# Fifteen filler products from a tile set by DVE, in place of ten that need POOL's identity

## What is computed

```python
# x: (8, 128, 32, 32); Wq, Wk: (64, 128); Wv: (128, 128)
xf = x.reshape(b, c, n)                                  # n = 1024 pixels
q = einsum('oc,bcn->bon', Wq, xf) + bq[None, :, None]
k = einsum('oc,bcn->bon', Wk, xf) + bk[None, :, None]
v = einsum('oc,bcn->bon', Wv, xf) + bv[None, :, None]
attn = softmax(einsum('bci,bcj->bij', q, k), axis=-1)
out = einsum('bcn,bmn->bcm', v, attn)
return gamma * out + x
```

## Time and profile before

| what | us |
|---|---|
| median of 3 runs | 231.02 |
| lowest and highest of them | 230.31, 231.49 |
| the profiled execution's own time | 231.92 |
| its span, first to last instruction | 230.1 |
| PE busy | 223.4 (97% of the span) |
| ACT, POOL, DVE busy | 177.9, 189.1, 168.2 |
| mean granted clock of TensorE | 0.999 |

### The profile page before, as it was taken

The page is one execution under the profiler, slowest core; times in us unless marked ns, Lnnn a source line. Parts: engine busy times, 40 slices in busy tenths (PEclk is TensorE's granted clock), DMA queues, the critical chain, the costliest instruction groups (busy, mean ns, idle before and its releaser), DMA issues.

```text
span 230.1 us, 5324 instructions
## 1 busy us (share of the span) xinstructions
PE 223.4 (97%) x1858; PEld 204.8 (89%) x1858; DVE 168.2 (73%) x339; ACT 177.9 (77%) x342; POOL 189.1 (82%) x163
## 2 busy tenths in 40 slices
PE   7999989999999999999999999999999999999994
PEld 4477868999999999999999999999999999999994
DVE  0586869976878878868897778768887777776544
ACT  2578967777887888877887788878887878878980
POOL 8668888696998979987798979989799878799871
PEclk9999999999999999999999999999999999999999
DMA  5571940096406770195504961076302951100111
GB/s 151 143 265 28 203 137 4 2 229 166 157 3 160 159 231 0 15 232 133 178 0 93 226 171 63 2 184 141 140 0 35 231 153 43 47 0 3 46 50 46
DMA packets 17978, 24.56 MB, mean 107 GB/s; under 512 B 9760, under 2 KB 10784, under 8 KB 17952
## 3 DMA queue, kind: packets, MB, share of 16 engines
q1 hardware_dynamic: 17520, 24.03, 40.9%
q10 hardware_dynamic: 432, 0.20, 0.3%
HBM read 8.72 MB, written 4.19 MB: 56 GB/s over the span
## 4 chain that ended last, share of the span: by engine, by line
PE 88%; DVE 5%; ACT 2%; DMA 2%; issue 1%; SPq 1%; POOL 0%; POOLq 0%; ACTq 0%
PE sums L612 24%; PE scores L592 13%; PE scores L593 12%; PE work L548 12%; PE sums L626 12%; PE work L542 5%; DMA k_hilo<-qk_lo 2%; DVE neg_max L840 2%; PE work L535 1%; PE scores L641 1%; PE work L537 1%; PE work L536 1%; PE work L641 1%; PE sums L632 1%; DVE weight_lo L878 1%
## 5 line engine op out<-in xcount | busy, mean ns | idle before, releaser
L469 POOL TENSOR_TENSOR weight_lo<-weight,weight_hi 128x512 bf16<-128x512 f32 x97 | 134.9, 1406 | 22.3 <-ACT weight_hi L779 21.5
L840 DVE TENSOR_REDUCE neg_max<-work 128x1 f32<-128x512 f32 x120 | 81.4, 683 | 4.7 <-PE work L548 4.7
L776 ACT ACTIVATE weight<-scores 128x512 f32<-128x512 f32 x128 | 76.7, 599 | 9.5 <-PE scores L593 1.8
L612 PEld LDWEIGHTS sums<-values,weight_hi 128*128 128x128 f32 x504 | 76.8, 189 | 5.0
L612 PE MATMUL sums<-values,weight_hi 128*128 128x258 f32 x504 | 80.7, 282 | 0.0
L779 ACT ACTIVATE weight_hi<-scores 128x512 fp32r<-128x512 f32 x128 | 76.8, 600 | 0.0
L592 PE MATMUL scores<-q_hihi,k_hilo 128*128 128x256 f32 x256 | 71.0, 300 | 0.2 <-ACT q_lomax L760 0.2
L593 PE MATMUL scores<-q_lomax,k_hione 128*128 128x256 f32 x256 | 66.2, 281 | 0.0
L548 PE MATMUL work<-k_hilo,q_hihi 128*128 128x512 f32 x120 | 49.0, 413 | 0.8 <-DVE neg_max L840 0.5
L592 PEld LDWEIGHTS scores<-q_hihi,k_hilo 128*128 128x128 f32 x256 | 48.2, 188 | 1.6 <-issue 0.9
L593 PEld LDWEIGHTS scores<-q_lomax,k_hione 128*128 128x128 f32 x256 | 48.5, 189 | 1.1 <-issue 0.5
(11 more groups left out here) (72 smaller groups left out, 158.4 us busy)
## 6 DMA issues: line engine op xcount, KB each, us to landing
x_turned_sb<-in_x_turned SPq DMA_DIRECT2D x8, 512.0 KB, 5.0
out<-y_sb SPq DMA_DIRECT2D x15, 256.0 KB, 2.7
x_sb<-in_x SPq DMA_DIRECT2D x7, 512.0 KB, 4.4
q_hihi<-qk_hi SPq DMA_DIRECT2D x12, 256.0 KB, 4.4
q_lomax<-qk_lo SPq DMA_DIRECT2D x7, 256.0 KB, 5.7
k_hione<-qk_hi SPq DMA_DIRECT2D x7, 256.0 KB, 5.6
k_hilo<-qk_hi SPq DMA_DIRECT2D x6, 256.0 KB, 3.2
k_hilo<-qk_lo SPq DMA_DIRECT2D x6, 256.0 KB, 5.7
```

Of the source, the lines that this page charges most:

```text
L469: pool.tensor_tensor(weight_lo[:, r], weight[:, r], weight_hi[:, r], ALU.subtract).then_inc(weight_lo_pool_done, 1)
L612: last = pe.matmul(sums[:, u % 2 * PAIR + it, 0:VCOLS], weight_hi[:, r, part_tile(kt, it)], values[p][:, key_tile(s, kt)], start=(j == 0 a ...
L776: act.activation(weight[:, r], scores[:, s % 2], ACT.Exp)
L840: dve.reduce_max(neg_max[:, t, h:h + 1], place, AX.X, negate=True).then_inc(neg_max_done, 1)
```

## The change

The ten transposes of `identity` become fifteen plain fp32 products, each `filler.T @ filler` over 128 columns. `filler` is a new 128x128 fp32 tile of ones. DVE sets it with a memset ahead of everything else that it does, and counts a new semaphore, `filler_set`. PE's first wait is for that semaphore in place of POOL's second setup step. The fillers write the same PSUM place as before, which nobody reads before it is overwritten. POOL's setup, ACT's use of the identity and all that follows the fillers stay as they are.

```diff
-WARM_UP = 10
+WARM_UP = 15
...
         identity = sbuf("identity", [128, 128], fp32)
+        filler = sbuf("filler", [128, 128], fp32)
...
+        filler_set = sem("filler_set")
...
             def keep_busy(turns, place):
                 for _ in range(turns):
-                    pe.transpose(place[:, 0:128], identity[:, :], identity[:, :])
-
-            pe.wait_ge(pool_setup, IDENTITY_MADE)
+                    pe.matmul(place[:, 0:128], filler[:, :], filler[:, :], start=True, stop=True)
+
+            pe.wait_ge(filler_set, 1)
             keep_busy(WARM_UP, sums[:, 0])
...
+            dve.memset(filler[:, :], 1.0).then_inc(filler_set, 1)
             dve.wait_ge(biases_loaded, 16)
```

## The result

| | before | after |
|---|---|---|
| median, us | 230.86 (6 runs) | 232.43 (6 runs) |
| lowest to highest, us | 230.31 to 231.96 | 231.89 to 232.83 |
| ratio after to before | | 1.0058, 95% interval 1.0034 to 1.0082 |
| profiled execution: time, span | 231.92, 230.1 | 231.89, 230.1 |

The change costs 1.57 us by the medians, and 1.3 us (0.8 to 1.9) by the ratio. The two profiled executions show next to none of it: 231.92 and 231.89 us. Why that is so is the main thing to learn here. It has two parts: the moment at which TensorE's clock rose, and 0.25 us that the changed kernel does not lose at 107 us (under "Hidden elsewhere").

A forecast was written before the change was run, and what follows sets the result against it. PE bounds the kernel, busy 97% of the span. k0 starting 3.48 us later, less 2.06 us for six shorter passes, gives +1.42 us on the median 231.02: 232.4 us, range 230.9 to 233.1.

The forecast's parts named there:

- Hidden elsewhere: Rival: k0 late, but the stretch from 10 to 16 us gives most back; about 231.0 us, chance 0.08.
- The start: Head: DVE's memset, begun at 0.73, lets the first filler start at 0.98 instead of 1.52, 0.54 us earlier.
- The passes: Fillers on PE: fifteen fp32 products are 30 passes, 0.2125 us each cold, 6.38 us if all are cold.
- The rise: TensorE's clock doubles at 7.33 us; all 30 fillers cold to 7.36, six warm passes to 9.94, +1.42 us.
- the one lag of the trace: Head: the clock rises 6.35 us behind the first filler, transposes included, so at 7.33 after the change.
- the rival: Head: only plain products count for the clock, which rises at 4.97; +0.27 us, 231.3 us, chance 0.32.
- Two signs of failure: Head and end: the clock rises before 4.4 us, or the delay at k1 is not found again at the end.
- Profiled executions: Whole kernel: profiled 231.92 us would become 233.34; the median of the runs, 0.90 lower at 231.02, becomes 232.4.
- The argument against the rival: Head: the profiled execution, rise at 7.87, was slowest of four; 230.31 would mean a rise at about 4.7.
- theory A: Head: every PE pass, transposes too, counts for the clock; its rise varies between executions; loss is the 30 passes' time.
- theory B: Head: only plain products count for the clock, transposes do not; as a rival of the forecast 231.3 us, chance 0.32.
- the faster rival: Fillers: a product costs one pass, not two; 229.7 us; chance 0.08 together with a rise before 4.4 us.

The follow-up runs named there:

- e4: The changed kernel with its 15 fp32 products made one-pass (bf16, 256 columns): 230.72 us, ratio 0.9981 to the kernel before.
- e5: The changed kernel with 13 one-pass bf16 products instead of 15 fp32 ones: 230.57 us, ratio 0.9967 to the kernel before.
- e12: The changed kernel with PE's old wait for POOL's identity added, 15 fp32 products: 232.87 us, ratio 1.0093 to the kernel before.
- e2: The kernel before with ten fp32 products in place of its ten transposes, still waiting for POOL: 232.22 us, ratio 1.0049.
- e13: The changed kernel with 7 fp32 products instead of 15 and PE's old wait for POOL's identity added: ratio 1.0007 to the kernel before.
- e6: The changed kernel with 30 fp32 products instead of 15: 237.36 us, ratio 1.0282 to the kernel before.
- e7: The kernel before, unedited and profiled once more: 231.76 us, against 231.92 in its first profile.
- e1: The kernel before without any filler: 232.06 us, ratio 1.0039.
- e11: The changed kernel with ten one-pass bf16 products, waiting also for POOL's identity as the kernel before did: ratio 1.0014 to the kernel before.

## Why the prediction was right

**The start.** DVE's memset began at 0.83, not at 0.73, and took 0.17 us; the first filler came at 1.05 where I said 0.98 (bounds 0.88 to 1.13). Nothing on DVE was delayed. Right, and small.

**The passes.** Line 634 shows x30, cold 0.213 us apart and warm 0.11, as worked out from the earlier trace rows. e4 and e5 show that the second pass of each product is what the change loses. e12, e2 and e13 give its price: from 7 to 15 products behind POOL the ratio goes from 1.0007 to 1.0093, 2.0 us for 16 passes, 0.12 us each.

**The rise.** Here the working was right in its kind and wrong in one step. I took the one lag of the trace, 6.35 us, for a constant, and so had all 30 passes cold and k0 at 7.36. The profile of after shows k0 at 6.1 to 6.25, which I had named as the sign of the rival (only plain products count). By the test that I had set, the rival had won, and its time of 231.3 was wrong. The test was bad, since the rise lay between 3.2 and 6.3 us behind the first pass in the traces of this study. Two signs of failure that I had named were touched as well: the rise came at 4.40 us, at the bound of 4.4, and the 0.14 us by which k1 is late in this trace (8.84 instead of 8.70) is not found again at the end (span 230.06 instead of 230.12).

The total came out all the same, because the lag hardly enters it. I had not worked that out, so this part was luck. With a lag L behind the first pass, k1 is through at 5.26 + L / 2 in the kernel before: the cold passes would end at 3.88 + 6 x 0.853 = 9.0, and half of what lies behind the rise at 1.52 + L is spared. In the changed kernel the fillers end at 1.05 + L + (30 - L / 0.213) x 0.112 = 4.41 + 0.475 L, and six warm passes lead to 6.99 + 0.475 L. The difference is 1.73 - 0.025 L: 1.65 us at a lag of 3.2 and 1.57 at 6.3. Less the 0.25 us that the main loop gives back (under "Hidden elsewhere") it is 1.3 to 1.4 us; the ratio gives 1.3 (0.8 to 1.9), and the medians differ by 1.57. I had 1.42, from one lag and a start at 0.98, and without the 0.25 us: the head was sized 0.15 to 0.2 us too small and the loop's part was left out, and the two nearly cancel.

**Profiled executions.** I set the sum on the profiled 231.92 and moved it to the median. That was sound, but the 0.90 us between them need not be the cost of profiling: a rise at 7.86 is near the late end, and 231.92 near the highest of before. The argument against the rival, that this execution was the slowest of the four, was the right reading. The profiled execution of after is the other extreme, the lowest of its six.

**Hidden elsewhere.** Up to 50 us nothing is: the 0.14 us by which v's projection is later in the first profile of after is found again at 47 us (k_hilo's transfer stands in the chain at 47.04 instead of 46.90), and e6 carried 3.64 us through to 50 us. But 0.25 us comes back at one place of the main loop, which the sum took as equal in both kernels. First the kernel before, then the changed one (timeline of DVE, POOL and PEld, and the chain of PE):

```profile
104.30 1.28 POOL L469 TENSOR_TENSOR weight_lo<-weight,weight_hi 128x512 bf16<-128x512 f32 x1
104.57 1.57 DVE L878 TENSOR_TENSOR weight_lo<-weight,weight_hi 128x512 bf16<-128x512 f32 x1 [0.29 <-ACT weight_hi L779]
107.19 0.97 PEld L542 LDWEIGHTS work<-w_v_t,x_sb 128*128 128x128 f32 x8 [0.21 <-DVE neg_max L840]
107.19 1.15 PE work L542 x8
```

```profile
104.30 0.69 DVE L880 TENSOR_TENSOR weight_lo<-weight,weight_hi 128x512 bf16<-128x512 f32 x1
104.40 1.74 POOL L471 TENSOR_TENSOR weight_lo<-weight,weight_hi 128x512 bf16<-128x512 f32 x1
107.31 0.89 PE work L544 x8
```

In the kernel before, DVE's `weight_lo` starts behind POOL's and takes 1.57 us, its next `neg_max` starts at 106.46, and PE waits for it. In the changed kernel DVE's `weight_lo` starts first and takes 0.69 us, and `neg_max` starts at 105.75. All traces divide in this way: POOL starts first, and PE's passes at this place take 1.06 to 1.16 us, in the four without the new tile (before, its repeat e7, e1, e2); DVE starts first, and they take 0.89 us, in the ten with it. Between 100 and 112 us PE gains 0.23 to 0.26 us on the first trace of before in eight of these ten, 0.14 in e4 and 0.08 in e13. So the ratio of every version with the new tile holds a gain that has nothing to do with the clock or the number of passes, and e5's -0.8 us is one of them. What in the edit turns the order of the two engines was not tried. One ratio fits worse with it: e11's head must then be about 0.5 us slower than that of the kernel before (0.2 to 0.9), where theory A gives 0.05. This stays open; it speaks against theory B all the more. The chance of 0.41 for a loss beyond 0.5% is neither borne out nor refuted by 0.58% (0.34 to 0.82); the faster rival was rightly near zero.

## What to carry to other kernels

Count fillers in passes and in microseconds, not in calls: an fp32 product is two passes, a transpose or a bf16 product one, and whatever lies behind the landing of the first operands is paid. Before comparing two profiles of a short difference, read in each at what moment the pace of PE's passes doubled; where that moment differs, compare medians of many runs, or work both out to the same rise. Compare two traces to their ends, and not only where the edit is: here as much as a sixth of the loss came back at a place 100 us behind it. An effect of which the only sign is one profiled rise needs a run without the cause (here: no filler) over many executions.

## What was not expected

- In fourteen profiled executions, with fillers or without, the rise lay 3.2 us (e12: 4.79 behind a start at 1.61) to 6.3 us (before: 7.86 behind 1.52) after PE's first pass. The times of the kernel before scatter over 230.33 to 231.96 in 35 runs, 1.6 us, which is about half of that spread of 3.1 us.
- Ten transposes, 2.4 us of work that nobody reads, are worth 0.9 us (e1), because PE has nothing else to do while it waits for the k weights; passes beyond the landing of the k weights cost more than they give (e2 against the kernel before, the change against e4).
- A head that was 3.64 us later ended 5.1 us later (e6), since one transfer took 6.37 instead of 4.96 us.
- A new tile and one memset ahead of everything change the order of DVE and POOL at 104 us in the main loop, and with it 0.25 us.
